# Cross attention in runs: score pairs grouped by two, whole jobs between them, maxima in double banks, exponentials in single ones

## The reference

```python
def _L1_xattn_ref(Q, K, V, mask, Wq, bq, Wk, bk, Wv, bv, Wo, bo):
    q = _split_heads(Q @ Wq.T + bq)
    k = _split_heads(K @ Wk.T + bk)
    v = _split_heads(V @ Wv.T + bv)
    scores = jnp.einsum('bhqd,bhkd->bhqk', q, k) / jnp.sqrt(jnp.float32(D_K))
    scores = jnp.where(mask[:, None, :, :] == 0, NEG_INF, scores)
    attn = jax.nn.softmax(scores, axis=-1)
    out = jnp.einsum('bhqk,bhkd->bhqd', attn, v)
    return out.transpose(0, 2, 1, 3).reshape(B, S, H * dk) @ Wo.T + bo
x = x + _L1_xattn_ref(_layernorm(x), ctx_1024, ctx_1024, mask_BxSxS2_if1, ...)
```

## Time and profile before

| | |
|---|---|
| three runs, median (lowest, highest) | 2679.61 us (2673.09, 2679.92) |
| the profiled execution's own time | 2676.99 us |
| its span | 2675.3 us |
| mean granted TensorE clock | 0.95 |
| PE / PEld / DVE / ACT / POOL busy | 2173.0 / 1393.3 / 1511.9 / 909.7 / 839.0 us |
| maxima of the cross attention (L1114) | 544 x 687 ns, 361.0 us |
| exponentials (L1026) | 256 x 1027 ns, 261.6 us |
| score matmuls (L889, L903) | 544 x 502 ns, 512 x 466 ns |

### The profile page before, as it was taken

How to read it: one execution, slowest core, us unless ns; L and a number is a source line. 1 busy time by engine, 2 the same in 40 slices (tenths; PEclk the granted TensorE clock), 3 DMA queues, 4 the chain that set the end, 5 groups by cost and what they waited for, 6 DMA issues and landing times. The chain is left out here.

```text
span 2675.3 us, 37634 instructions
## 1 busy us (share of the span) xinstructions
PE 2173.0 (81%) x11961; PEld 1393.3 (52%) x11961; DVE 1511.9 (57%) x2569; ACT 909.7 (34%) x1283; POOL 839.0 (31%) x753
## 2 busy tenths in 40 slices
PE   2340899999999405999999999838999999999997
PEld 1340899999999402333333333624554544554554
DVE  7820454545554343666676666644656656656655
ACT  2410333333333200455555555312333333333332
POOL 0067553425550362122112221111323323333332
PEclk9999999999999756899999999669999999999998
DMA  3162332333322322232332223324223223223322
GB/s 126 68 238 99 111 119 80 112 122 118 118 75 67 108 85 88 88 92 92 88 104 73 93 92 94 112 56 95 63 70 86 66 68 87 68 64 87 72 60 59
DMA packets 149073, 244.69 MB, mean 91 GB/s; under 512 B 22503, under 2 KB 71311, under 8 KB 146699
## 3 DMA queue, kind: packets, MB, share of 16 engines
q1 hardware_dynamic: 107650, 163.52, 21.9%
q0 software_dynamic: 11104, 44.06, 4.8%
q10 hardware_dynamic: 30272, 36.53, 4.3%
HBM read 120.48 MB, written 67.04 MB: 70 GB/s over the span
## 5 line engine op out<-in xcount | busy, mean ns | idle before, releaser
L1114 DVE TENSOR_REDUCE ca_negmax<-ca_na 128x1 f32<-128x512 f32 x544 | 361.0, 687 | 143.2 <-PE ca_na L889 142.7
L1026 ACT ACTIVATE ca_pr<-ca_st 128x1024 f32<-128x1024 f32 x256 | 261.6, 1027 | 230.8 <-PE ca_st L903 230.8
L889 PE MATMUL ca_na<-ca_k_stack,ca_q_stack 64*128 64x512 f32 x544 | 251.7, 502 | 20.8 <-DVE ca_negmax L1114 11.9
L592 DVE TENSOR_TENSOR ex_h<-ex_up,ex_sg 128x512 f32<-128x512 f32 x136 | 94.0, 692 | 305.7 <-ACT ex_sg L555 198.0
L1713 DVE TENSOR_REDUCE sa_negmax<-sa_na 128x1 f32<-128x512 f32 x272 | 182.7, 674 | 130.7 <-PE sa_na L1534 126.4
L515 PE MATMUL ex_gp<-ex_xp,moe_gu_p 128*128 128x256 f32 x1632 | 221.9, 286 | 1.8 <-DVE ex_xp L578 1.4
L903 PE MATMUL ca_st<-ca_q_stack,ca_k_stack 64*128 64x512 f32 x512 | 218.8, 466 | 0.0
L528 PE MATMUL ex_yp<-moe_dn_p,ex_hp 128*128 128x256 f32 x1632 | 209.0, 286 | 12.0 <-DVE ex_hp L582 12.0
L515 PE MATMUL ex_up<-ex_xp,moe_gu_p 128*128 128x256 f32 x1632 | 218.7, 284 | 0.0
L515 PEld LDWEIGHTS ex_gp<-ex_xp,moe_gu_p 128*128 128x128 f32 x1632 | 206.1, 193 | 3.0 <-DVE ex_xp L578 1.8
L528 PEld LDWEIGHTS ex_yp<-moe_dn_p,ex_hp 128*128 128x128 f32 x1632 | 198.8, 191 | 16.0 <-DVE ex_hp L582 16.0
(11 more groups left out here) (261 smaller groups left out, 3821.8 us busy)
## 6 DMA issues: line engine op xcount, KB each, us to landing
sa_q<-sa_qh SPq DMA_DIRECT2D x140, 128.0 KB
sa_k<-sa_kh SPq DMA_DIRECT2D x140, 128.0 KB
ex_raw_m<-masks ACTq DMA_DIRECT2D x34, 512.0 KB, 3.9
moe_gu_raw<-gateupT POOLq DMA_DIRECT2D x8, 2048.0 KB, 8.2
ca_q_stack<-q_parts SPq DMA_DIRECT2D x216, 64.0 KB
ca_k_stack<-k_parts SPq DMA_DIRECT2D x216, 64.0 KB
expert_rows<-rt_zeros SPq DMA_DIRECT2D x20, 512.0 KB, 15.7
k_parts<-ca_kp SPq DMA_DIRECT2D x9, 1024.0 KB, 5.6
```

Of the source, the lines that this page charges most:

```text
L889: pe.matmul(na[s % 2][:, :], q_stack[g][rows, i, t * P:(t + 1) * P], k_stack[g][rows, i, :], start=not masked, stop=True).then_inc(na_full, 1)
L1026: act.activation(pr[:, pair // 2 % 2, h:h + 2, :], st[pair % 2][:, :, :], ACT.Exp, scale=DK ** -0.5).then_inc(exp_done, 1)
L1114: dve.tensor_reduce(negmax[:, g % 2, 1 - s % 2, s // (2 * TB), s // 2 % TB:s // 2 % TB + 1], na[s % 2][:, :], AX.X, ALU.max, negate=True). ...
```

## The change

Slots are grouped into runs of two (`RUNS` = 8 a unit). In a run PE does two pairs of `score_b` and `score_a`; behind it may stand a value visit (behind runs 0, 2, 4, 6) and a whole job. Pieces are gone. The jobs get new places, o0 and o1 in g3 instead of g1. Within a run both `score_a` lie in one half of the array and both `score_b` in the other, and the halves change from run to run (the heads' order in `pr` follows). `na` is two of two banks with one reduction of 1024 elements a run; `st` is two of one bank with one exponential of 512 a slot. The four DMAs of a unit's rows are issued by SP, between the bias loads, the stores and the stack loads, instead of by ScalarE.

```diff
-        na = [m.ps(f"na{i}", [P, S]) for i in range(2)]
-        st = [m.ps(f"st{i}", [P, 2, S]) for i in range(2)]
+        na = [m.ps(f"na{i}", [P, 2, S]) for i in range(2)]
+        st = [m.ps(f"st{i}", [P, S]) for i in range(2)]
...
-        JOBS = [("m", 0, 0), ("k0", 0, 3), ("k1", 0, 6), ("xT0", 0, 8), ("xT1", 0, 10), ("n0", 0, 11), ("rv", 0, 12),
-                ("q0", 0, 15), ("m", 1, 0), ("q1", 1, 3), ("t0", 1, 4), ("t1", 1, 6), ("o0", 1, 10), ("n1", 1, 11), ("o1", 1, 15),
-                ("m", 2, 1), ("v0", 2, 7), ("n2", 2, 9), ("v1", 2, 14), ("m", 3, 1), ("n3", 3, 10)]
-        PIECES = {"m": 1, "k": 2, "x": 1, "r": 1, "q": 2, "v": 4, "o": 4, "n": 1, "t": 1}
+        JOBS = [("m", 0, 0), ("k0", 0, 1), ("n0", 0, 2), ("k1", 0, 3), ("xT0", 0, 4), ("xT1", 0, 5), ("rv", 0, 6), ("q0", 0, 7),
+                ("m", 1, 0), ("q1", 1, 1), ("t0", 1, 2), ("t1", 1, 3), ("n1", 1, 4),
+                ("m", 2, 0), ("v0", 2, 1), ("n2", 2, 2), ("v1", 2, 5),
+                ("m", 3, 0), ("n3", 3, 2), ("o0", 3, 3), ("o1", 3, 7)]
...
+            def send_rows(g, a):
+
+                sp.wait_ge(ml_ready, a + 1)
+                for r in range(2):
+                    for j in range(2):
+                        row = j * HALF + RM + r
+                        sp.dma_start(q_stack[g][row:row + 1, :, :].bitcast(F32).rearrange("a i (t n) -> a (i t) n", n=P),
+                                     mrow[j * 2 * TB:(j + 1) * 2 * TB, r, :].bitcast(F32)).then_inc(m_in, 16)
...
                 load_bias(nxt(b), (b + 1) % 2)
+                send_rows(1, b * G + 1)
                 store(kp, k_parts, misc_free, k_stored, b * nj + (nf + number("k1") + 1))
+                send_rows(2, b * G + 2)
                 store(qp, q_parts, qp_ready, q_stored, b * KC + 2 * KC)
                 for g in range(G):
...
                     load_stack(g)
+                    if g == 1:
+                        send_rows(3, b * G + 3)
                     if g == 2:
                         load_context(sp, io, ctxT, ctx_in, (b + 2) % B)
+                        send_rows(0, b * G + 4)
...
+                r, t, i, j = s // 2, s // HG, s % 2, 1 - s // 2 % 2
+                rows = slice(j * HALF, (j + 1) * HALF)
...
+                if i == 0:
+                    pe.wait_ge(max_done, a * RUNS + r + 1)
...
+                pe.wait_ge(exp_done, u * SLOTS + s + 1)
...
-                        for s in range(SLOTS):
-                            score_b(g, b, s, u, masked)
-                            score_a((g + 2) % G, b if g < 2 else b + 1, s, u + 2, masked)
-                            if s == 2:
-                                pe.wait_ge(exp_done, u * (SLOTS // 2) + 2)
+                        for r in range(RUNS):
+                            for s in (2 * r, 2 * r + 1):
+                                score_b(g, b, s, u, masked)
+                                score_a((g + 2) % G, b if g < 2 else b + 1, s, u + 2, masked)
+                            t = r // 2 - 1
+                            if r == 0:
+                                pe.wait_ge(exp_done, u * SLOTS + 2)
                                 values((g - 1) % G, TB - 1)
-                            elif s > 3 and s % 4 == 3:
...
+                            elif r % 2 == 0:
+                                pe.wait_ge(exp_done, u * SLOTS + (HG * t + HG + 2))
...
-                            for n, name, piece in pieces_at(g, s):
+                            for n, name in jobs_at(g, r):
...
-                        if s == 8:
-                            send_rows((g + 1) % G, u + 1)
...
+                            act.activation(pr[:, s // HG % 2, s % HG, :], st[s % 2][:, :], ACT.Exp, scale=DK ** -0.5).then_inc(exp_done, 1)
...
+                dve.tensor_reduce(negmax[:, g % 2, 1 - r % 2, :, r // 2], na[r % 2][:, :, :], AX.X, ALU.max, negate=True).then_inc(max_done, 1)
```

More of the change, by code:

```diff
@@ L743, in cross_attention, with jobs_at @@
         nj, nf = len(JOBS), len(FIRST)
[L745 to L752, removed]
+        def jobs_at(g, r):
+            return [(n, j[0]) for n, j in enumerate(JOBS) if j[1:] == (g, r)]
         def number(name):
@@ L824, in max_rows, with output @@
                 bank_free(n)
-                pe.wait_ge(max_done, a * SLOTS + SLOTS + 2)
+                pe.wait_ge(max_done, a * RUNS + RUNS + 2)
                 pe.transpose(misc[0:HG * TB, 0:P], negmax[:, par, :, :, :].rearrange("p j i t -> p (j i t)"), ident[:, :]).then_inc(misc_full, 1)
[L828 to L836, removed]
+            def output(n, c):
+                bank_free(n)
+                for t in range(2):
+                    tok = (2 * c + t) * P
+                    for i in range(KC):
+                        last = pe.matmul(misc[:, t * D:(t + 1) * D], outT[:, i, tok:tok + P], wo[:, i, :], start=(i == 0), stop=(i == KC - 1))
+                last.then_inc(misc_full, 1)
             def queries(n, u):
@@ L862, in prepare @@
                 elif name[0] == "k":
-                    if piece == 0:
-                        pe.wait_ge(ctx_in, b * 16 + 16)
-                    last = pe.matmul(misc[:, :], wk[:, piece, c * P:(c + 1) * P], ctxT[:, piece, :], start=(piece == 0), stop=(piece == KC - 1))
+                    pe.wait_ge(ctx_in, b * 16 + 16)
+                    for i in range(KC):
+                        last = pe.matmul(misc[:, :], wk[:, i, c * P:(c + 1) * P], ctxT[:, i, :], start=(i == 0), stop=(i == KC - 1))
                 elif name[0] == "x":
@@ L870, in prepare @@
                 elif name[0] == "q":
[L871 to L877 removed]
+                    for i in range(KC):
+                        last = pe.matmul(misc[:, :], wq[:, i, c * P:(c + 1) * P], xT[:, i, :], start=(i == 0), stop=(i == KC - 1))
+                else:
+                    for t in range(2):
+                        tok = (2 * c + t) * P
+                        for i in range(KC):
+                            last = pe.matmul(misc[:, t * D:(t + 1) * D], ctxT[:, i, tok:tok + P], wv[:, i, :], start=(i == 0), stop=(i == KC - 1))
+                last.then_inc(misc_full, 1)
             def score_a(g, b, s, a, masked):
[L881 removed]
+                r, t, i, j = s // 2, s // HG, s % 2, 1 - s // 2 % 2
+                rows = slice(j * HALF, (j + 1) * HALF)
                 if s == 0:
@@ L892, in score_b @@
+                last = pe.matmul(na[r % 2][:, i, :], q_stack[g][rows, i, t * P:(t + 1) * P], k_stack[g][rows, i, :],
+                                 start=not masked, stop=True)
+                if i:
+                    last.then_inc(na_full, 1)
             def score_b(g, b, s, u, masked):
-                t, i, rows = s // HG, s % HG // 2, slice(s % 2 * HALF, (s % 2 + 1) * HALF)
-                pair = s // 2
+                t, i, j = s // HG, s % 2, s // 2 % 2
+                rows = slice(j * HALF, (j + 1) * HALF)
@@ L904, in score_b @@
-                if s % 2:
-                    last.then_inc(st_full, 1)
+                    pe.matmul(st[i][:, :], ident16[:, :], nbT[:, b % 2, t, :], start=True, stop=False)
+                pe.matmul(st[i][:, :], k_stack[g][rows, i, t * P:(t + 1) * P], q_stack[g][rows, i, :],
+                          start=not masked, stop=True).then_inc(st_full, 1)
             def values(g, t):
                 for h in range(HG):
-                    last = pe.matmul(av[32 * h:32 * h + 32, :], vw[:, g, t, h, :], pr[:, t % 2, h, :],
+                    last = pe.matmul(av[32 * h:32 * h + 32, :], vw[:, g, t, h, :], pr[:, t % 2, h % 2 * 2 + h // 2, :],
@@ L952, in _ @@
                     pe.wait_ge(set_up, SETUP)
-                for piece in range(PIECES[name[0]]):
-                    prepare(n, name, 0, piece)
+                prepare(n, name, 0)
             for t in range(TB - 1):
@@ L969, in _ @@
                 else:
-                    for piece in range(PIECES["o"]):
-                        output(n, B, int(name[1]), piece)
+                    output(n, int(name[1]))
         @block.scalar
@@ L1010, in _ @@
                     evacuate(n, name, 0)
-            send_rows(0, 0)
             with act.Fori(0, B) as b:
@@ L1167, in _ @@
             for g in range(2):
-                for s in range(SLOTS):
-                    maximum(g, s, g)
+                for r in range(RUNS):
+                    maximum(g, r, g)
             with dve.Fori(0, B) as b:
```

71 lines of the change are left out of this document (24 added, 47 removed).

## The result

| | median (lowest to highest), runs | its profiled execution |
|---|---|---|
| kernel before | 2672.6 us (2668.9 to 2679.9), 16 | 2677.0 us |
| changed kernel | 2668.9 us (2663.5 to 2675.1), 16 | 2665.3 us |

A forecast was written before the change was run, and what follows sets the result against it. TensorE (PE) was taken as the full engine, with g1 set by a DMA chain. Profiled 2677.0 + 0.8 (loop) - 3.6 (prologue) = 2674.2 us; the median lies 2.6 above: 2677, range 2658 to 2699.

The forecast's parts named there:

- The mechanism: g1: a DMA chain of 16.6 us from q1's end to g2 sets its length; PE idles 5.3 us (the hold).
- Rival 4: g1: the chain does not hold it, g1 is 15.6 and the clock stays; 2615 us, chance 0.03.
- The moved jobs: o0, o1 leave g1 for g3: PE work outside the chain goes from 51.6 to 52.6 us a batch.
- The clock: g2, after the hold: about 4.8 us at low clock, costing 2.0 us (1.3 to 2.8) each batch.
- Rival 1: g2: the hold costs no clock, or it is regained at once; 2661 us, chance 0.23.
- Rival 2: g2: low clock stands 10 us after each hold, each batch loses 4.5 us; 2697 us, chance 0.20.
- Unit walk: Steady batch: g2 16.1, g3 16.8, g0 19.8, g1 to q1's end 4.8, chain 16.6; sum 74.1 us before clock cost.
- bare runs' waits: Runs without a visit wait for exponentials, about 0.85 us each; four lie outside the chain, in g2 and g3.
- Widths: Maxima of 1024 take 1.22 us, exponentials of 512 take 0.60; VectorE goes from 52 to about 47 us a batch.
- cost 0: Rows' DMAs on SP: they land in time for every unit, with margins of about 4 us, so no cost.
- signs of being wrong: Profile after: gap under 3 us, PE's clock 1.00 through g2, or a unit's b0 waiting for ca_mrow's DMA.
- 3.6 saved: Prologue: two units of maxima take 1.35 us instead of 1.57, 16 times; bounds 0 to 5.

The follow-up runs named there:

- e1: Changed kernel with output jobs o0 and o1 back in g1 instead of g3; 2639.0 us, ratio to the kernel before 0.9865.
- e4: Changed kernel with the key and zero parts of stack 0 loaded ahead of q's store; 2633.4 us, ratio to the kernel before 0.9857.
- e2: Changed kernel with six extra matmuls of 128x512, result unread, at the end of g1; 2652.0 us, ratio to the kernel before 0.9915.
- e5: Kernel before with only its row DMAs issued by SP, at the changed kernel's places; 2670.2 us, ratio to the kernel before 0.998.
- e7: Changed kernel with o0, o1 in g1, stack 0's key and zero parts loaded early, first rows sent before stack 3's load; 2599.2 us, ratio 0.9714.
- e8: e7 plus one spare one-element exponential at the head of each batch, for an early table load; 2601.4 us, ratio to the kernel before 0.9709.
- e9: Changed kernel plus one spare one-element exponential at the head of each batch, for an early table load; 2659.3 us, ratio 0.9936.
- e6: Changed kernel with both widths undone: maxima of 512 in single banks, exponentials of 1024 in double banks; 2681.9 us, ratio 1.0021.
- e3: Changed kernel with the rows' DMAs issued by ScalarE again, ahead of run 4; 2694.0 us, ratio to the kernel before 1.0076.

## Why the prediction came out right, and where its steps did not

**The mechanism held: the DMA chain sets g1.** Predicted: g1 up to q1's end 4.8 and a chain of 16.6, a hold of 5.3. Measured 4.56, 16.47 and 5.71. e1 adds 3.5 us of PE work to g1 and it lasts as long; e4 shortens the chain and it shrinks. Rival 4 is out.

**The moved jobs.** The prediction had g3 at 16.8, 3.0 longer than before, and placed the savings of PE work in g1, where they are worth nothing. g3 is 16.05, and e1 gives 2.8 of it back. This is where the saved work went: PE is busy for 6.0 us less in g1 (14.36 instead of 20.37), and the hold is 5.7 where PE had stood still for about 0.3.

**The clock.** 2.0 a batch predicted, 2.4 measured (e2 against after, g2 alone). Rival 1 (no cost) is out. Rival 2 had the right length and the wrong price: the clock does stand low for 10.24 us a batch, but it falls 1.4 us into the hold, so only 5.85 us of work are slow. It had priced all ten as work. In the forecast's own term, 4.8 us of low clock were put where 5.85 followed; halved, less what waits cover, these give the 2.4. Its range of 3.4 to 6.8 doesn't follow from the earlier trace rows, which show 4.5 (the same trace does have low stretches of 3.41 and 6.83 us elsewhere). And one piece of its evidence doesn't hold: it took the low stretch of the earlier trace rows as the cost of a hold of 0.92. That stretch begins 1.77 us after the hold is over, and no hold of 0.5 to 1.1 us in e2, e5, e7 or e8 was followed by one; what lowered the clock there isn't shown. (The Trainium skill, TensorE: Matmul & The Clock Gate, HAM oscillation, says that waits for DMA between bursts of matmuls drop the clock each time; in the changed kernel the trace agrees, in all 8 batches. In e1, with holds of about 3.0 us, it failed to drop once, and in e4, with 1.9, twice.)

**Unit walk.** At full clock g2 is 15.35 (predicted 16.1), g3 16.05 (16.8), g0 20.22 (19.8). The bare runs' waits were taken too high: g2 has 0.96 of idle PE (15.35 less 14.39) where 1.6 were put, g3 1.15 where 2.3 were. g0 has a wait that the prediction doesn't name, the table load's (1.0 by e9). In the kernel before, the load ran at once when the last exponential had ended, ahead of a copy that was next in ScalarE's program:

```profile
1308.92 1.02 ACT L1026 ACTIVATE ca_pr<-ca_st 128x1024 f32<-128x1024 f32 x1 [0.18 <-PE ca_st L903]
1309.97 1.28 ACT L981 ACT_TABLE_LOAD   x1
1311.26 0.26 ACT L981 COPY ca_mfull<-ca_misc 16x128 f32<-16x128 f32 x1
```

In the changed kernel an exponential is next, with its wait for scores, and the load stands behind that. (The Trainium skill, ScalarE: Activation LUTs, Table-load gate, says that the load stands right before the activation that needs it and takes some 2.7 us with its drain; the place agrees in the changed kernel, where an exponential follows, while in the kernel before a copy does; the price doesn't: from 1309.97 to 1311.26 it is 1.29.) The sum is 75.05 instead of 76.1: from the first score pair to the stage's last matmul the time fell by 4.3 us, where + 0.8 was forecast. The + 0.8 itself leans on the 75.90 of the earlier trace rows; from the true mean of 75.5 the same walk gives + 0.6 a batch and + 4.0 in all, so the loop was missed by more than it seems.

**Widths.** The two durations were right (1.22 and 0.60). What they bring is 0.8 us a batch, net of the clock (e6).

**Rows by SP: "cost 0" failed in the prologue.** The loop's margins held, no steady unit waits for rows, and ScalarE's relief is worth 3.1 a batch in the new order. But the first rows stand behind all the stack loads of the prologue, and one of the prediction's own signs of being wrong, a unit's first score pair that waits for `ca_mrow`'s DMA, came true once:

```profile
1070.20 2.72 SPq L785 DMA_DIRECT2D ca_q_stack<-ca_mrow  x4
...
1074.19 0.79 PE L915 MATMUL ca_st<-ca_q_stack,ca_k_stack 64*128 64x512 f32 x1 [3.01 <-DMA ca_q_stack<-ca_mrow]
```

So of 3.6 saved only 1.1 arrive (24.65 against 25.79). The saving itself was there, 4.4 us in e3 (21.43) and e7 (21.42), in which the rows go early. (The Trainium skill, TensorE: Matmul & The Clock Gate, Packing small matmuls, says that a weight load overlaps only matmuls in other row groups, which would have left a saving of 2. The trace disagrees: of two maxima in the same half, the second's weight load starts at 1054.78, while the first runs from 1054.61 to 1055.40 (matmul ends are modelled in the profile), and 4.4 were saved.) The prediction walked the queue of SP for the steady batch and not for the first one. This + 2.5 and the loop's - 5.1 cancel in part: that the sum came out nearer than its terms is luck.

**The balance of the parts**, for one batch: before 75.5; rows by SP - 0.9 (e5, 74.6); order, grouping and moved jobs + 1.3 (e6, 75.9); widths - 0.8 (after, 75.1). Each of these steps takes in what the clock did in it. The moved jobs are the dear term in the + 1.3: with o0 and o1 back in g1 the batch is 71.1 (e1), 4.0 less.

## To carry to other kernels

Find the stretch whose length a DMA chain sets, and fill it with work before saving any: a job moved out of it costs most of its time (2.8 of 3.8 us here), a microsecond saved in it turns into idle time, and that can cost clock too. When an edit moves issues to another engine's queue, walk that queue once for the steady loop and once for the first pass. Shortening the chain pays in full only until PE fills the stretch, so shorten and fill together, as e7 does.

## What the runs showed of the hardware

- Idle time before a unit can be dearer than work: 5.4 us of useless matmuls in the hold saved 2.4 us a batch (e2, 15.35 instead of 17.75 in g2).
- Whether a short hold costs clock varied between batches of one execution: 1.74 to 1.95 us of hold in e4 were followed by low stretches of 3.4 us, none, none, 3.4 and four times 6.8; holds of about 3.0 in e1 by 6.8 once, 3.4 six times and none once; those of 5.7 to 5.8 us (7.2 in the first batch) by 10.24 in every batch of the changed kernel, but by 6.83 in three of e9; those of 0.9 to 1.1 in e2 by none.
- Four issues by ScalarE held its exponentials for 2.2 us (e3). They cost 3.1 us a batch in the changed kernel and 0.9 in the kernel before (e5); these two differ in the exponentials' banks and in the order of work, and no run separates the two.
